# One change in two places: the even class's scores in three products, and the first norm's root once per batch

## The reference

```
def attention(Q, K):                   # 8 heads of 256 channels, each channel by itself; values are K
    corr = ifft(fft(q) * conj(fft(k))).real          # over the 512 positions
    w, idx = top_k(corr, 12);  w = softmax(w)
    out = sum_i w[i] * v[min(idx[i] + pos, 511)]
x = x + attention(layernorm(x), ctx)
h = layernorm(x)
x = x + h @ W.T + bias + lora(h)       # 16 experts of rank 16, weighted by coeffs * scales
```

## Time and profile before

| | us |
|---|---|
| runs of the kernel before | 2602.17, 2594.43, 2596.8 |
| their median | 2596.8 |
| the profiled execution | 2623.54 |
| its span, first to last instruction | 2621.7 |
| granted TensorE clock, mean over the span | 0.980 of full speed |

### The profile page before, as it was taken

One profiled execution on the slowest core, in us unless ns is written; L12 is line 12 of the kernel. 1 busy time (PEld: TensorE's weight loads), 2 busy tenths in 40 slices (PEclk: granted clock), 3 DMA queues, 4 the chain that ended last, 5 costly groups with the idle time before them and its releaser, 6 DMA issues.

```text
span 2621.7 us, 36204 instructions
## 1 busy us (share of the span) xinstructions
PE 2458.5 (94%) x12288; PEld 1534.9 (59%) x12288; DVE 1942.5 (74%) x4526; ACT 1090.8 (42%) x2070; POOL 2069.6 (79%) x1430
## 2 busy tenths in 40 slices
PE   4999866899999979999999999997999999999999
PEld 3666555566666646666666666664666666654444
DVE  5888889778887798778887788779886788645000
ACT  4888856543444333543444344442433344211000
POOL 5799999778998779978997899788797889654222
PEclk8999978899999989999999999998999999999999
DMA  9399998967897677967897689966786687768853
GB/s 328 100 266 270 272 251 199 232 200 223 275 271 211 220 235 236 279 203 225 273 282 209 222 266 284 270 190 203 228 257 183 213 262 246 200 225 288 266 184 113
DMA packets 550025, 613.17 MB, mean 234 GB/s; under 512 B 322640, under 2 KB 448720, under 8 KB 532176
## 3 DMA queue, kind: packets, MB, share of 16 engines
q1 hardware_dynamic: 549840, 610.86, 77.8%
HBM read 383.22 MB, written 151.00 MB: 204 GB/s over the span
## 4 chain that ended last, share of the span: by engine, by line
PE 60%; POOL 16%; DMA 7%; DVE 6%; issue 5%; SPq 4%; ACT 2%; POOLq 0%; DVEq 0%; ACTq 0%
PE f_ps L834 12%; PE f_ps L836 12%; PE f_ps L838 12%; PE a_ps L706 8%; PE a_ps L751 4%; PE a_ps L799 3%; POOL f_x1p L1126 3%; PE a_ps L814 3%; PE a_ps L815 3%; POOL a_zu L1126 2%; POOL a_rows L1126 2%; POOL a_zvf L1126 2%; DMA a_w_lag<-a_w_row 2%; PE a_ps L756 1%; DVE a_twf L1251 1%
## 5 line engine op out<-in xcount | busy, mean ns | idle before, releaser
L834 PE MATMUL f_ps<-f_whi,f_hhi 128*128 128x512 f16 x2048 | 777.1, 379 | 5.8 <-issue 2.3
L836 PE MATMUL f_ps<-f_wlo,f_hhi 128*128 128x512 f16 x2048 | 776.9, 379 | 0.0
L838 PE MATMUL f_ps<-f_whi,f_hlo 128*128 128x512 f16 x2048 | 776.5, 379 | 0.0
L1126 POOL TENSOR_TENSOR a_zvf<-a_zvf,a_twf 128x512 f32<-128x512 f32 x256 | 340.6, 1361 | 115.8 <-DVE a_twf L1251 110.1
L918 ACT ACTIVATE a_side<-a_ps 128x1 f32<-128x1 f32 (+2 forms) x420 | 123.2, 331 | 543.6 <-PE a_ps L795 368.7
L838 PEld LDWEIGHTS f_ps<-f_whi,f_hlo 128*128 128x128 f16 x2048 | 200.6, 98 | 242.2 <-issue 1.1
L836 PEld LDWEIGHTS f_ps<-f_wlo,f_hhi 128*128 128x128 f16 x2048 | 200.6, 98 | 225.3 <-issue 0.8
L834 PEld LDWEIGHTS f_ps<-f_whi,f_hhi 128*128 128x128 f16 x2048 | 200.8, 98 | 219.7 <-issue 5.9
L1126 POOL TENSOR_TENSOR f_x1p<-f_x1p,f_y 128x512 f32<-128x512 f32 x128 | 170.9, 1368 | 100.1 <-DVE f_y L1251 100.1
L918 ACT ACTIVATE a_vu<-a_ps 128x512 f32<-128x512 f32 (+2 forms) x512 | 218.4, 489 | 73.4 <-PE a_ps L706 72.8
L751 PE MATMUL a_ps<-a_w_lag,lags 128*128 128x256 f16 x1536 | 234.8, 277 | 12.7 <-DMA a_w_lag<-a_w_row 11.5
(11 more groups left out here) (134 smaller groups left out, 5054.8 us busy)
## 6 DMA issues: line engine op xcount, KB each, us to landing
f_whi<-whi_scratch SPq DMA_DIRECT2D x128, 512.0 KB, 5.0
f_wlo<-wlo_scratch SPq DMA_DIRECT2D x128, 512.0 KB, 5.9
a_rows<-in_x_dram SPq DMA_DIRECT2D x62, 1024.0 KB, 8.6
vs<-in_ctx_dram SPq DMA_DIRECT2D x64, 512.0 KB, 6.2
xs<-in_x_dram SPq DMA_DIRECT2D x64, 512.0 KB, 7.6
parts_scratch<-a_so SPq DMA_DIRECT2D x64, 512.0 KB, 7.5
x_scratch<-a_rows SPq DMA_DIRECT2D x32, 1024.0 KB, 5.1
f_x1p<-x_scratch SPq DMA_DIRECT2D x32, 1024.0 KB, 6.6
```

The lines of the kernel that those rows point to most:

```text
L834: nc.tensor.matmul(f_ps[:, t, :], h_hi[q][:, kq, rows_t], w_hi[u % WR][:, :, kq, :], start=(k == 0), stop=False)
L836: nc.tensor.matmul(f_ps[:, t, :], h_hi[q][:, kq, rows_t], w_lo[u % WR][:, :, kq, :], start=False, stop=False)
L838: mm = nc.tensor.matmul(f_ps[:, t, :], h_lo[q][:, kq, rows_t], w_hi[u % WR][:, :, kq, :], start=False, stop=(k == DB - 1))
L1126: return nc.gpsimd.tensor_tensor(whole, whole, part, op)
```

## The change

Two edits. First, in the 50 chunks of `halved_odd` the even class is no longer two products of 256 columns per group. Two products of 129 columns, accumulated, make lags 0 to 128; a third of 127 columns, by a new matrix with twice the sines, makes what lags 129 to 255 differ by from their mirror images. ACT copies these 127 columns to SBUF, into the part of `a_w_row` that the weights take later (`twice_sines`); before the first such copy ACT waits until the previous chunk's weights have been turned. DVE subtracts them from lags 1 to 127, a third instruction beside L1307 and L1308. The new matrix (128x127, f32, 65 KB) is loaded at the start, behind `inv`.

Second, the first norm's root is no longer taken for one tile at a time, between the upper and the lower products. It is taken once for a batch's four tiles, in windows 5 (batch 1), 13, 21, 29, 37, 45 and 53 (batches 2 to 7), behind `weights_low` and so in front of `tile_scale`, `row_statistics` and `part_output`: 15 instructions on 128x4, each on two SBUF tensors; three constants, `eps4`, `three_halves` and `bits4`, are filled at the start. Each waits for the one before it by a semaphore.

```diff
@@ transform_matrices
     inv[0, 0, 0] /= 2
+    sines = 2 * inv[0, 1, :, 1:T]
+    sines[0] = 0
     inv[0, 1, 0] = np.cos(np.pi * lag) / L
@@ Shared.load_matrices
-        for name, dst in (("inv", self.inv), ("lags", self.lags), ("ident16", self.ident16), ("out", self.outm)):
+        for name, dst in (("inv", self.inv), ("sines", self.sines), ("lags", self.lags), ("ident16", self.ident16), ("out", self.outm)):
@@ flow
+        def closed_batch(w):
+
+            if w == 5:
+                return 1
+            return (w - 13) // CHUNKS + 2 if w >= 13 and (w - 13) % CHUNKS == 0 and (w - 13) // CHUNKS < BATCH - 2 else None
...
+        def twice_sines(g):
+
+            return w_row[:, 1, g, :].bitcast(F32)[:, 1:T]
@@ TensorE, correlate
                     for cls in range(2):
+                        if cls == 0 and halved_odd(n):
+                            for k in range(2):
+                                nc.tensor.matmul(corr[:, g, 0:T + 1], prod[:, 2 * k, g * T:(g + 1) * T],
+                                                 inv[:, 0, k, 0:T + 1], start=(k == 0), stop=(k == 1))
+                            nc.tensor.matmul(corr[:, g, T + 1:2 * T], prod[:, 2, g * T:(g + 1) * T],
+                                             shared.sines[:, :], start=True, stop=True)
+                            continue
@@ TensorE, ahead of window 0
-            pe.wait_ge(shared.const_in[1], 16 * 4)
+            pe.wait_ge(shared.const_in[1], 16 * 5)
@@ ScalarE, the normalising of a chunk
-                at_least(act, stat_done, TB * (n // CHUNKS))
+                at_least(act, stat_done, n // CHUNKS)
@@ ScalarE, part_corr
                 at_least(act, out_moved, n - 1)
+                if halved_odd(n):
+                    at_least(act, w_turned, 2 * (n - dma_turns(n)))
+                    at_least(act, w_dma, 32 * dma_turns(n))
                 for g in range(SUB):
                     act.wait_ge(corr_mm, SUB * n + g + 1)
                     if halved_odd(n):
+                        copy(twice_sines(g), corr[:, g, T + 1:2 * T])
                         copy(side[:, g, T:2 * T], corr[:, g, 3 * T:4 * T])
@@ VectorE, part_corr
                         nc.vector.tensor_tensor(near, sines, far, ALU.subtract)
-                        nc.vector.tensor_tensor(far, sines, far, ALU.add).then_inc(odd_joined, 1)
+                        nc.vector.tensor_tensor(far, sines, far, ALU.add)
+                        nc.vector.tensor_tensor(corr[:, g, T + 1:2 * T], corr[:, g, 1:T], twice_sines(g), ALU.subtract
+                                                ).then_inc(odd_joined, 1)
                         dve.wait_ge(odd_joined, odd_joins(n) + g + 1)
@@ VectorE, close_statistics
             def close_statistics(w):
 
-                m = stats_tile(w - 1)
-                if m is None:
+                of = closed_batch(w)
+                if of is None:
                     return
-                gain, column = stat[:, (m // TB + 1) % 2, :, m % TB:m % TB + 1], slice(m % (2 * TB), m % (2 * TB) + 1)
-                dve.wait_ge(rows_done, m + 1)
-                at_least(dve, stat_done, m)
-                nc.vector.tensor_scalar(s_veps[:, :], squares[:, column], 1.0 / D, EPS, ALU.mult, ALU.add
-                                        ).then_inc(var_done, 1)
-                dve.wait_ge(var_done, m + 1)
-                inverse_root_of_tile(nc, dve, s_veps[:, :], s_root[:, :], s_sq[:, :], gain[:, 0, :], 1.0, root_link,
-                                     TILE_LINKS * m).then_inc(gain_done, 1)
-                dve.wait_ge(gain_done, m + 1)
-                nc.vector.tensor_scalar(gain[:, 1, :], minus_mean[:, column], gain[:, 0, :], None, ALU.mult
+                first = TB * (of - 1) % (2 * TB)
+                gain, columns = stat[:, of % 2, :, :], slice(first, first + TB)
+                dve.wait_ge(rows_done, TB * of)
+                dve.wait_ge(q_normed, CHUNKS * (of - 1))
+                link, base = root_link, ROOT_LINKS * (of - 1)
+                nc.vector.scalar_tensor_tensor(out=s_veps[:, :], in0=squares[:, columns], scalar=1.0 / D, in1=eps4[:, :],
+                                               op0=ALU.mult, op1=ALU.add).then_inc(link, 1)
+                dve.wait_ge(link, base + 1)
+                nc.vector.scalar_tensor_tensor(out=s_root[:, :].bitcast(I32), in0=s_veps[:, :].bitcast(I32), scalar=-0.5,
+                                               in1=bits4[:, :], op0=ALU.mult, op1=ALU.add).then_inc(link, 1)
+                for i in range(3):
+                    at = base + 4 * i
+                    dve.wait_ge(link, at + 2)
+                    nc.vector.tensor_tensor(s_sq[:, :], s_root[:, :], s_veps[:, :], ALU.mult).then_inc(link, 1)
+                    dve.wait_ge(link, at + 3)
+                    nc.vector.tensor_tensor(s_sq[:, :], s_sq[:, :], s_root[:, :], ALU.mult).then_inc(link, 1)
+                    dve.wait_ge(link, at + 4)
+                    nc.vector.scalar_tensor_tensor(out=s_sq[:, :], in0=s_sq[:, :], scalar=-0.5, in1=three_halves[:, :],
+                                                   op0=ALU.mult, op1=ALU.add).then_inc(link, 1)
+                    dve.wait_ge(link, at + 5)
+                    nc.vector.tensor_tensor(gain[:, 0, :] if i == 2 else s_root[:, :], s_root[:, :], s_sq[:, :], ALU.mult
+                                            ).then_inc(link, 1)
+                dve.wait_ge(link, base + ROOT_LINKS)
+                nc.vector.tensor_tensor(gain[:, 1, :], minus_mean[:, columns], gain[:, 0, :], ALU.mult
                                         ).then_inc(stat_done, 1)
 
@@ VectorE, ahead of window 0
+            nc.vector.memset(eps4[:, :], EPS)
+            nc.vector.memset(three_halves[:, :], 1.5)
+            nc.vector.memset(bits4[:, :], ROOT_BITS)
@@ VectorE, a window
                     tile_scale(2 * w - 3)
-                close_statistics(w)
...
                     weights_low(w)
+                close_statistics(w)
                 if w == 0:
```

More of the change, by code:

```diff
@@ L41 @@
 ROOT_BITS = 0x5F3759DF
-LINKS, TILE_LINKS = 12, 9
+LINKS, TILE_LINKS, ROOT_LINKS = 12, 9, 14
 def position_order():
@@ L92, in transform_matrices @@
     return {"fold": fold.transpose(1, 0, 2), "lags": np.stack([high, low], axis=1), "inv": inv.transpose(2, 0, 1, 3),
+            "sines": sines,
             "out": out.transpose(1, 0, 2), "ident": np.eye(T), "ident16": np.eye(T).astype(np.float16)}
@@ L164, in __init__ @@
         self.inv = sb("inv", [T, 2, 2, 2 * T])
+        self.sines = sb("sines", [T, T - 1])
         self.outm = sb("outm", [T, 4, T])
@@ L264, in flow @@
         root = sb("a_root", [T, TB])
-        s_veps, s_root, s_sq = (sb(f"a_s_{name}", [T, 1]) for name in ("veps", "root", "sq"))
+        s_veps, s_root, s_sq, eps4, three_halves = (
+            sb(f"a_s_{name}", [T, TB]) for name in ("veps", "root", "sq", "eps4", "three_halves"))
+        bits4 = sb("a_s_bits4", [T, TB], I32)
         rows_but_0 = sb("a_rows_but_0", [T, 1])
@@ L355, in flow @@
         rows_done = sem("a_rows_done")
-        var_done = sem("a_var_done")
         root_link = sem("a_root_link")
-        gain_done = sem("a_gain_done")
         stat_done = sem("a_stat_done")
```

## The result

The changed kernel takes 2642.7 us (median of 4 runs, 2637.75 to 2646.08) for 2599.49 (4 runs): ratio 1.0152, with a 95% interval of 1.0099 to 1.0205, or +43 us. The forecast was +32.0, 2628.8, with 2592 to 2650 as its range.

The account below looks back on a forecast made before the run. PE was taken to bound the 50 product windows, POOL to stand nearest to full in the preparing ones. The terms -13.8 + 42.5 + 2 + 1 + 0.3 gave +32.0 us, 2628.8 for the median, range 2592 to 2650.

Parts of the forecast that it names:

- the held links: Late closings: small instructions (links) reading two SBUF tensors don't run beside POOL instructions; 8.5 us each in five windows, +42.5.
- the even class: Product windows: fewer columns on PE win 0.43 us in 32 of 50 windows, -13.8 us (between 0 and -21.6).
- Rival A: Late closings: the links (small closing instructions) are not held, PE waits for nothing; sum -21, 2576 us; chance 0.16.
- The columns: Scores on PE: time follows columns, 129 and 127 at 0.109 us each; 0.43 us less per window.
- The early place: Per-tile closings removed from DVE: nothing won in product windows; about 1.5 us won per window in 2 to 8.
- so there I count nothing won: 18 of 50 product windows, where PE already waits on turned weights: no gain from the shorter products counted.
- Windows 2 to 13: 2 to 4 win 1.5 us each, 5 loses 14.2, 6 to 8 win 2.5 each: +2; window 13: +1.
- Rival B: Row windows: the small closing instructions are held, but long row splits go; 2594 us, or 2611 with one; chance 0.15.
- rival C: Row windows: the shift makes long row splits come oftener, two more than before; +35, 2664 us; chance 0.08.

Follow-up runs that it names:

- close_psum: Changed kernel, but in five product windows the closing's intermediate values lie in PSUM, one instruction more: 2603.32 us, ratio 1.0019 to the kernel before.
- close_only: Changed kernel with only the once-per-batch closing, the even class as before: 2644.57 us, ratio 1.0161 to the kernel before.
- even_only: Changed kernel with only the new even-class products, the first norm closed per tile as before: 2604.25 us, ratio 1.0024 to the kernel before.
- second profile of before: The kernel before, unchanged, profiled once more, one run: 2598.03 us, longest row split 5.5 us.
- before_turns: Kernel before, with the weight-turning DMAs issued ahead of the rows' store and next attention load in windows with a rows tile: 2574.19 us, ratio 0.9909.
- even_turns: New even-class products alone, weight-turning DMAs issued ahead of the rows' store and next attention load: 2555.42 us, ratio 0.9849 to the kernel before.
- best: New even class, weights turned first, batches 3 to 7 closed once per batch through PSUM, 1 and 2 per tile: 2556.64 us, ratio 0.9858 to the kernel before.

## Why the prediction was right, step by step

The way and most of the size came from the step on the held links, and that step was right. The sum was still 16 us short of what the two profiles without long splits give (+32.0 for +48.05), almost all of it in one term that came out beyond its own bounds, the even class. The measured 2642.7 lies within 8 us of the top of the range, so that the range took this in was luck in part.

**The links are held: right, and shown.** The step from three rows to "does not run beside a POOL instruction" carried +42.5; the five windows gave 38.2. PE's wait was 5.0 us (25.2 in five) for 6.5. Five links came through before the bias and the sixth lasted almost as long as it, so nine were left behind it for the 12 forecast (0.2 us each, 0.6 in all); and POOL came to the bias's end 24.1 us after the scores for 24.6. What the windows lost beyond the wait, the lower clock, was (38.2 - 25.2) / 5 = 2.6 us per closing for 2.0. The Trainium skill ("SBUF — State Buffer", section "Who interferes with whom") says of a VectorE instruction with two SBUF inputs and a GpSimd one that reads SBUF that whichever issues first has the ports that the two share for its whole instruction. The trace agrees for the links, whose longest hold, 4.42 us, ends with one POOL instruction, a bias of 4.49. It does not for the row split of 20.05 us, which lay over twelve.

**Rival A falls**: beside POOL's work the links follow every 0.2 us only when they do not read two SBUF tensors, as in `close_psum`. Its time, 2576, needed unheld links and no new waits on the weights; each failed.

**The columns: right.** Products of 129, 127 and 128 columns all take 0.11 us an instruction from start to start; 35.08 for 35.46 is 0.38, for 0.43. The first group's scores of window 20 in after:

```profile
729.32 0.61 PE L808 MATMUL a_ps<-inv,a_prod 128*128 128x129 f32 x4
729.76 0.39 PE L810 MATMUL a_ps<-sines,a_prod 128*128 128x127 f32 x2
729.99 0.39 PE L814 MATMUL a_ps<-inv,a_prod 128*128 128x128 f32 x2
```

**The early place: right where it can be told.** The undisturbed windows of `close_only` take 35.46 us, as before.

**The even class's sum: the term that was mis-sized.** The step "so there I count nothing won", on three of every eight windows, gave -13.8, between 0 and -21.6. In those 18 windows the change did not win nothing, it lost: 44.0 us beyond the undisturbed length for 22.8. So the whole edit came to -18.6 + 21.2 = +2.6, outside the bounds.

The working looked at when the weights end, and put that 0.33 us later. They end 0.07 us sooner, 15.77 us after the scores for 15.84. But what PE waits for is the DMA that turns them, and it stands in SP's queue behind one or two transfers that wait for POOL's rows. PE wants the turned weights 23.8 us after the scores for 24.2, and that queue does not move when PE gets faster: in window 34 the turning starts 18.15 us after the scores in `even_only`, 17.13 in the second profile of before, and PE gets the weights 28.08 us after them for 25.99. That they come even later there is why the waits grew by more than the 0.4 us; why they come later is open. By `before_turns` this queue had cost the kernel before some 20 us already.

The longer waits also cost the clock. In window 26 of after the granted clock was 0.57 in the 4 us behind a wait of 2.00 us, and the window was 3.84 us longer; in window 60 it stayed at 1.00 behind one of 1.86, and the window was 2.03 longer.

**Windows 2 to 13: right in sign, short in size.** Windows 2 to 4 take 32.35 us for 33.0 to 34.1, 3.3 us won in sum for 4.5. Window 5 became longer by just the forecast 14.2 us (47.7 for 33.5), and there the number was luck: the links were held as forecast, but it was not the queries that waited first. It was the products for the experts' part, on DVE's sums of `p_w` behind the closing.

```profile
PE f_ps L881 <- DVE p_w L1501: 9.8, 1, 9.8
```

Windows 6 to 8 won 1.5 each for 2.5, and window 13 lost 3.0 for 1. In sum, up to the scores of window 14, +7.9 against the first profile of before and +4.7 against the second, for +3. The +2.8 us from window 63 on were not forecast and are open; the two profiles of before differ there by 1.5.

**Rival B came true in the profiles and not in the medians.** No profile of the six kernels with the new even class, after among them, held a long split, and rival C did not show. The median of before already held few, so their loss shows between the first profile of before and that of after, where windows 26 and 50 of before were 35.3 us too long. That the splits are gone from the runs is not shown: one run of six of `even_turns` and two of six of `best` lie 12 us and more over all the others. Whether, and why, long splits became rarer was not tried.

## What to carry to other kernels

A small instruction is not cheap by its size: ask which of its operands lie in SBUF, what GpSimd does at that moment and for how long in one instruction, and put one operand into PSUM, as `close_psum` did, where the answer is "for long". Before taking columns off TensorE, list the waits that end last in each kind of window, and look up what stands ahead of the releasing DMA in its queue: here the gain was given back there, and more with it, until the order in that queue was changed. And where a profile and the median of the runs differ by 1%, find the event that makes the difference before sums are made on it.

## What the runs showed of the hardware

- A held link is let through at the end of the POOL instruction beside it, and at times one more passes before POOL's next: in window 21 the link of 783.04 took 0.16 us where POOL's rows lie 0.08 us apart, and the next one was held.
- The 128x2048 split of 933.92, on two SBUF tensors, was held over twelve POOL instructions. The first eleven boundaries between them overlap in the rows by 0.07 or 0.08 us. The split ended at 953.97, 2.1 us behind the first boundary with a gap, and there POOL's next instruction took 3.20 us where its like take 1.3:

```profile
950.53 1.29 POOL L1156 TENSOR_TENSOR a_tq<-xs 128x512 f32<-128x512 f32 x1
951.90 3.20 POOL L1160 TENSOR_TENSOR xs<-a_tq 128x512 f32<-128x512 f32 x1
```

The other two long splits, at 1808.38 in the same profile and at 1854.51 in that of `before_turns`, ended in the same way, at the first gap of 0.08 us. Shorter splits and small links also got through where POOL's rows overlap (a split of 3.35 us at 947.37 in after), so what makes a split long is not shown.
- The issue of the two turning DMAs took 4.36 us on SP's queue ahead of the rows' transfers and 7.37 behind them in window 34, for the same bytes. In the second of the four windows with rows it fell from 6.9 to 8.7 us to 3.8 to 6.5; in the fourth it did not fall in three windows of six.
